# Deviations of the row means made by TensorE and squared by ScalarE, in a convolution whose weights follow from the image

## The reference

```python
def _L0_conv_ref(x, w1, b1, fscale, conv_bias):
    avg = x.mean(axis=(2, 3))
    dyn = avg @ w1.T + b1
    wk = jax.nn.sigmoid(dyn).reshape(b * c, 1, K, K)
    y = lax.conv_general_dilated(xf, wk, ..., feature_group_count=b * c)
    y = y.reshape(b, c, h, w) + conv_bias[None, :, None, None]
    return (x - y) * fs * x + y

def _gn(v, G=32, eps=1e-05):      # one channel per group
    m = jnp.mean(g, axis=(2, 3, 4), keepdims=True)
    s = jnp.var(g, axis=(2, 3, 4), keepdims=True)
    return (g - m) / jnp.sqrt(s + eps)

x = x + _L0_conv_ref(_gn(x), ...)
```

## Time and profile before

| | us |
|---|---|
| median of 3 runs | 265.88 (265.69 to 266.33) |
| profiled execution | 265.87 |
| its span, first to last instruction | 263.9 |
| busy in it: TensorE | 235.7 (89%) |
| VectorE | 231.7 (88%) |
| GpSimd | 227.6 (86%) |
| ScalarE | 211.1 (80%) |

### The profile page before, as it was taken

One profiled execution on the slowest core, in us unless ns is written; L12 is line 12 of the kernel. 1 busy time (PEld: TensorE's weight loads), 2 busy tenths in 40 slices (PEclk: granted clock), 3 DMA queues, 4 the chain that ended last, 5 costly groups with the idle time before them and its releaser, 6 DMA issues.

```text
span 263.9 us, 9720 instructions
## 1 busy us (share of the span) xinstructions
PE 235.7 (89%) x3872; PEld 187.7 (71%) x3872; DVE 231.7 (88%) x552; ACT 211.1 (80%) x389; POOL 227.6 (86%) x259
## 2 busy tenths in 40 slices
PE   0069998989999999989999999999999999999991
PEld 0046875858788786878787887678787878888770
DVE  2886799999999999999999999899999999756655
ACT  2158789797898989797998989697989989899520
POOL 1261579899899999999999999999999999999982
PEclk9999999999999999999999999999999999999997
DMA  7999904696959989797979799797989733444476
GB/s 259 421 422 429 383 4 180 212 401 255 362 236 366 365 280 392 253 390 306 368 288 361 295 366 354 287 386 247 361 325 362 281 160 160 183 181 181 183 290 247
DMA packets 10413, 77.73 MB, mean 295 GB/s; under 512 B 1280, under 2 KB 1408, under 8 KB 2688
## 3 DMA queue, kind: packets, MB, share of 16 engines
q1 hardware_dynamic: 10368, 77.12, 75.8%
HBM read 39.37 MB, written 37.75 MB: 292 GB/s over the span
## 4 chain that ended last, share of the span: by engine, by line
PE 58%; DVE 23%; issue 10%; DMA 3%; ACT 2%; SPq 1%; POOL 1%; DVEq 0%; ACTq 0%; POOLq 0%
PE conv_ps L435 37%; PE conv_ps L441 13%; DVE outs L582 9%; DVE pieces L531 8%; DVE taps L549 4%; PE dyn_ps L419 3%; DMA w1s<-w1r 3%; PE dyn_ps L427 2%; PE conv_ps L497 1%; DVE taps L556 1%; ACT xs L686 1%; ACT linear L722 1%; DVE row_stats L538 1%; PE dyn_ps L404 1%; SPq L314 1%
## 5 line engine op out<-in xcount | busy, mean ns | idle before, releaser
L435 PE MATMUL conv_ps<-xs,taps 64*64 64x448 f32 x1536 | 219.9, 549 | 6.9 <-DVE outs L582 4.3
L852 POOL TENSOR_TENSOR outs<-outs,linear 128x1152 f32<-128x1152 f32 x63 | 166.1, 2647 | 1.0 <-DVE outs L582 0.7
L582 DVE SCALAR_TENSOR_TENSOR outs<-xs,beta,conv_ps 128x576 f32<-128x576 f32 x128 | 102.8, 805 | 20.3 <-PE conv_ps L435 19.6
L435 PEld LDWEIGHTS conv_ps<-xs,taps 64*64 64x64 f32 x1536 | 101.7, 133 | 26.6 <-issue 14.0
L441 PE MATMUL conv_ps<-xs,taps 64*64 64x128 f32 x1536 | 114.3, 272 | 0.6 <-issue 0.6
L722 ACT ACTIVATE linear<-xs,slope 128x576 f32<-128x576 f32 x128 | 109.0, 854 | 3.0 <-POOL outs L852 3.0
L531 DVE BATCH_NORM_STATS2 pieces<-xs 128x6 f32<-128x64 f32 (+1 forms) x256 | 102.2, 447 | 6.0 <-DMA xs<-x 6.0
L441 PEld LDWEIGHTS conv_ps<-xs,taps 64*64 64x64 f32 x1536 | 94.2, 133 | 9.3 <-issue 2.4
L686 ACT ACTIVATE xs<-xs,shift 128x594 f32<-128x594 f32 x128 | 99.2, 778 | 0.0
L809 POOL TENSOR_TENSOR inv_std<-numbers,minus_half 128x8 f32<-128x8 f32 x16 | 26.4, 1649 | 4.8 <-ACT dev_mean L692 4.6
L549 DVE TENSOR_TENSOR taps<-dyn_ps,tap 128x1512 f32<-128x1512 f32 (+1 forms) x19 | 27.8, 1477 | 0.0
(11 more groups left out here) (59 smaller groups left out, 142.0 us busy)
## 6 DMA issues: line engine op xcount, KB each, us to landing
xs<-x SPq DMA_DIRECT2D x30, 1188.0 KB, 11.2
out<-outs SPq DMA_DIRECT2D x30, 1152.0 KB, 5.2
xs<-x SPq DMA_DIRECT2D x4, 594.0 KB, 6.0
out<-outs SPq DMA_DIRECT2D x3, 576.0 KB, 2.8
out<-outs SPq DMA_DIRECT2D x2, 288.0 KB, 2.6
cst<-const SPq DMA_DIRECT2D x1, 275.5 KB, 6.9
w1s<-w1r SPq DMA_DIRECT2D x1, 144.0 KB, 6.8
gates<-gate SPq DMA_DIRECT2D x1, 8.0 KB, 7.0
```

Source lines behind the costliest of these rows:

```text
L435: return nc.tensor.matmul(tile(i, g, taken)[:, START:BANK], taps[given, i % 2, at:at + HALF], xs[given, i % XBUFS, g, 0:PAIRED, 1 + shift: ...
L582: nc.vector.scalar_tensor_tensor(out=outs[:, i % OBUFS, g].rearrange("p (k w) -> p k w", w=COLS), in0=xs[:, i % XBUFS, g, :, 1:1 + COLS], ...
L852: nc.gpsimd.tensor_tensor(tile, tile, linear[:, PAIR * k:PAIR * (k + 1)].rearrange("p g n -> p (g n)"), ALU.add).then_inc(out_ready, 1)
```

## The change

The table of constants gets one more 128 x 128 matrix, "deviate", which is the identity minus "average". Row means times this matrix are the deviations of the row means, so TensorE makes them beside the means: two matmuls more in `mean_even` and two in `mean_odd` (for images 0 and 1 one more over all partitions), into eight columns of PSUM next to the others. ScalarE copies them into `moments`, and squares them into `moments` with a second operation; `negative_mean` waits for the deviations now instead of for the means. The row variance is no longer added to the square: TensorE averages it by itself and accumulates it on the averaged squares, two more matmuls in `spread_even` and two in `spread_odd`. `second_moments` on GpSimd, with its three operations an image, is gone. Statistics lie variance behind mean (`row_stats` with the groups innermost). `mean_even` waits also until the second moments of the image before have been copied, since they share an accumulation region.

```diff
-for _name, _width in (("average", PARTS), ("band", TAPS * HALF), ("turn", TAPS),
+for _name, _width in (("average", PARTS), ("deviate", PARTS), ("band", TAPS * HALF), ("turn", TAPS),
...
+    put("deviate", np.eye(PARTS, dtype=np.float32) - same * new[:, None])
...
-        row_stats = sb("row_stats", [PARTS, 2, GROUPS, 2])
+        row_stats = sb("row_stats", [PARTS, 2, 2, GROUPS])
...
-        square = sb("square", [PARTS, GROUPS])
...
+        dev_ps = stat_ps[:, 3 * GROUPS:4 * GROUPS]
...
-        dev_ready = sem("dev_ready")
-        square_ready = sem("square_ready")
+        dev_done = sem("dev_done")
...
+            def deviate(rows, cols):
+                return const_of("deviate")[rows, cols]
             def mean_even(j):
...
+                pe.wait_ge(zstats_copied, 2 * j)
                 for cols in (TOP, BOTTOM):
-                    nc.tensor.matmul(stat_ps[cols, 0:GROUPS], average(TOP, cols), row_stats[TOP, j % 2, :, 0],
+                    nc.tensor.matmul(mean_ps[cols], average(TOP, cols), row_stats[TOP, j % 2, 0],
                                      start=True, stop=False).then_inc(mean_half, 1)
+                for cols in (TOP, BOTTOM):
+                    nc.tensor.matmul(dev_ps[cols], deviate(TOP, cols), row_stats[TOP, j % 2, 0],
+                                     start=False, stop=False).then_inc(mean_half, 1)
             def mean_odd(j):
-                pe.wait_ge(mean_half, 2 * (j - 1))
+                pe.wait_ge(mean_half, 4 * (j - 1))
                 for cols in (TOP, BOTTOM):
-                    nc.tensor.matmul(stat_ps[cols, 0:GROUPS], average(BOTTOM, cols), row_stats[BOTTOM, j % 2, :, 0],
-                                     start=False, stop=True).then_inc(mean_done, 1)
+                    nc.tensor.matmul(mean_ps[cols], average(BOTTOM, cols), row_stats[BOTTOM, j % 2, 0],
+                                     start=False, stop=False).then_inc(mean_done, 1)
+                for cols in (TOP, BOTTOM):
+                    nc.tensor.matmul(dev_ps[cols], deviate(BOTTOM, cols), row_stats[BOTTOM, j % 2, 0],
+                                     start=False, stop=True).then_inc(dev_done, 1)
             def spread_even(j):
-                pe.wait_ge(moments_ready, j + 1)
+                pe.wait_ge(moments_ready, 2 * (j + 1))
                 for cols in (TOP, BOTTOM):
-                    nc.tensor.matmul(stat_ps[cols, GROUPS:3 * GROUPS], average(TOP, cols),
-                                     moments[TOP].rearrange("p a g -> p (a g)"),
-                                     start=True, stop=False).then_inc(zstats_half, 1)
+                    nc.tensor.matmul(zstats_ps[cols], average(TOP, cols), moments[TOP].rearrange("p a g -> p (a g)"),
+                                     start=True, stop=False)
+                    nc.tensor.matmul(zstats_ps[cols, GROUPS:], average(TOP, cols), row_stats[TOP, j % 2, 1],
+                                     start=False, stop=False).then_inc(zstats_half, 1)
             def spread_odd(j):
...
                 for cols in (TOP, BOTTOM):
-                    nc.tensor.matmul(stat_ps[cols, GROUPS:3 * GROUPS], average(BOTTOM, cols),
-                                     moments[BOTTOM].rearrange("p a g -> p (a g)"),
+                    nc.tensor.matmul(zstats_ps[cols], average(BOTTOM, cols), moments[BOTTOM].rearrange("p a g -> p (a g)"),
+                                     start=False, stop=False)
+                    nc.tensor.matmul(zstats_ps[cols, GROUPS:], average(BOTTOM, cols), row_stats[BOTTOM, j % 2, 1],
                                      start=False, stop=True).then_inc(zstats_done, 1)
             def mean_whole(j):
...
-                nc.tensor.matmul(mean_ps, const_of("average"), row_stats[:, j % 2, :, 0],
-                                 start=True, stop=True).then_inc(mean_done, 1)
+                at_least(pe, zstats_copied, 2 * j)
+                nc.tensor.matmul(mean_ps, const_of("average"), row_stats[:, j % 2, 0],
+                                 start=True, stop=False).then_inc(mean_done, 1)
+                nc.tensor.matmul(dev_ps, const_of("deviate"), row_stats[:, j % 2, 0],
+                                 start=False, stop=True).then_inc(dev_done, 1)
             def spread_whole(j):
-                pe.wait_ge(moments_ready, j + 1)
+                pe.wait_ge(moments_ready, 2 * (j + 1))
...
-                                 start=True, stop=True).then_inc(zstats_done, 1)
+                                 start=True, stop=False)
+                nc.tensor.matmul(zstats_ps[:, GROUPS:], const_of("average"), row_stats[:, j % 2, 1],
+                                 start=False, stop=True).then_inc(zstats_done, 1)
...
-                    ins = nc.vector.bn_aggr(row_stats[:, j % 2, g, :], pieces[:, j % 2, g].rearrange("p h s -> p (h s)"))
+                    ins = nc.vector.bn_aggr(row_stats[:, j % 2, 0:2, g], pieces[:, j % 2, g].rearrange("p h s -> p (h s)"))
...
         def _(act):
-            act.wait_ge(ones_set, 1)
+            act.wait_ge(ones_set, 4)
...
             def negative_mean(j):
-                act.wait_ge(mean_done, j + 1 if j < 2 else 2 * j)
+                act.wait_ge(dev_done, j + 1 if j < 2 else 2 * j)
...
+                nc.scalar.activation(moments[:, 0], dev_ps, ACT.Identity).then_inc(moments_ready, 1)
+                nc.scalar.activation(moments[:, 1], dev_ps, ACT.Square).then_inc(moments_ready, 1)
...
-            def second_moments(j):
-                pool.wait_ge(rows_done, j + 1)
-                pool.wait_ge(neg_mean_ready, j + 1)
-                nc.gpsimd.tensor_tensor(moments[:, 0], row_stats[:, j % 2, :, 0], neg_mean_of(j),
-                                        ALU.add).then_inc(dev_ready, 1)
-                pool.wait_ge(dev_ready, j + 1)
-                nc.gpsimd.tensor_tensor(square[:], moments[:, 0], moments[:, 0], ALU.mult).then_inc(square_ready, 1)
-                pool.wait_ge(square_ready, j + 1)
-                nc.gpsimd.tensor_tensor(moments[:, 1], row_stats[:, j % 2, :, 1], square[:], ALU.add).then_inc(moments_ready, 1)
...
-            second_moments(0)
...
-            second_moments(1)
...
                 add_pair(i, 0)
...
-                if stats and i > 0:
-                    second_moments(i + 2)
...
                 add_pair(i, 1)
-                if i == 0:
-                    second_moments(2)
```

## The result

The changed kernel takes 273.78 us (median, 273.0 to 276.22) against 265.86 for the kernel before in the same comparison: 1.032 times as long, 95% interval 1.028 to 1.037. The forecast of 267.9 us had the sign and a quarter of the size, and its range ended at 270.2.

The account below looks back on a forecast made before the run. It took the bound to be a TensorE–VectorE loop of 14.44 us an image. Added: 0.88 (images 2 to 12), 0.1 (images 0, 1), 0.2 (image 13), 0.86 (start), 2.04 on 265.87: 267.9 us, range 266.2 to 270.2.

Parts of the forecast that it names:

- What bounds the kernel: Image loop of 14.44 us: TensorE to the end of tile 4, VectorE to product 5, then TensorE again.
- The price of the first four matmuls: Deviation matmuls on TensorE before tile 4's end: 0.08 us an image, bounds 0.04 and 0.25; 0.88 over images 2 to 12.
- The rival of the whole overhead: TensorE takes passes in order, each small one costing its whole overhead, 0.25 us an image: 270.1 us; chance 0.18.
- a steady image above 14.65: Sign in the profile after, mid-kernel image time in us, that would show the forecast wrong and whole overhead paid.
- The four spread matmuls: Row variances into second moments on TensorE behind tile 4: no loop cost, under about 0.4 us of cover.
- GpSimd's three operations at 0: Removing GpSimd's operations, 0.74 us an image, gains 0 in the middle, since no chain step stands behind them.
- the rival on it: GpSimd's 14.56 us an image was the long-run pace; freeing it removes long images, 266.6 us; chance 0.20.
- GpSimd's wait for ScalarE's copies: Sign in the profile after: GpSimd waits for ScalarE's copies before its power operation.
- ScalarE: Two added PSUM operations, 0.16 us each, counted at 0; idle before the negative mean falls from 1.2 to about 0.8.
- The start: Serial chain at the kernel's beginning takes all its additions: 0.86 us together, bounds 0 and 1.3.
- The second image's deviations: In the start, they stand on TensorE ahead of the first tile: 0.4 us more, bounds 0 and 0.53.
- The transfer of the weights: In the start, issued behind the constants table, which grows by 65.5 KB: 0.16 us later.

Follow-up runs that it names:

- e1: Kernel before with only the deviations' matmuls added (and the larger table of constants), nobody reading the deviations, GpSimd keeping its operations: 270.65 us.
- e2: Changed kernel without the four deviation matmuls in images 2 to 15, ScalarE using the means in their place: 265.71 us.
- e7: Kernel before with only one pair of deviation matmuls, behind the first pair of means, read by nobody: 270.97 us.
- v2: Kernel before with the dynamic-weight matmuls of images 3 to 15 moved to ahead of tiles 3 and 4: 265.39 us.
- e3: Changed kernel with the two pairs of deviation matmuls moved away from the means, into tiles 4 and 5, still ahead of product 4: 273.44 us.
- e4: Changed kernel with means and deviations in another order of array quarters, same places, each group of four using both row halves: 272.87 us.
- e8: Changed kernel with the first means and deviations half a tile earlier, ahead of the tile's first crossed pair: 271.25 us.
- v1: Changed kernel reworked: mean matmuls carry 32 columns, two added matmuls make deviations, spread matmuls as before, GpSimd regains one small operation: 270.09 us.
- v4: Shared 32-column mean passes with means, deviations and dynamic-weight matmuls moved to other tiles, GpSimd two operations fewer than the kernel before: 265.19 us.

## Why the prediction was wrong

**What bounds the kernel**: right for what was put ahead of product 4. TensorE to product 4, VectorE to product 5, TensorE again is the loop of e1, too, where TensorE waits 0.5 us for VectorE at the image's end. What was put ahead of product 4 lengthened every image by its full size, and e2 shows that nothing else in the change did.

**The price of the first four matmuls**: this is the step that failed, 0.08 forecast and 0.45 measured, eleven times, 4.95 us instead of 0.88. Its bounds, 0.04 and 0.25, came from rows in which small matmuls follow each other or stand one to a quarter, and both are prices per pass. The price here is not of the passes, as e7 shows: it is, by the reading above, mostly the time for which the queue stands until a 448-column pass has ended. The row that could have told it was in the trace of before, in the lines printed above: the mean that starts at 138.40 had waited for its quarter, and the order showed a second matmul for that quarter behind it. "The same instruction in the same place" was true and beside the point.

**The rival of the whole overhead** came nearer (270.1, and 0.18 of the chance), and its sign came, a steady image above 14.65, but for a wrong reason. TensorE does not take all passes in order, as it had it: two passes from behind the waiting mean start at 138.03, ahead of it. The rule of the Trainium skill in "TensorEngine Tiling (Array Packing)", section "Instruction Overhead", some 60 cycles a matmul, would have made the second pair cost as much as the first. Between e7 and e1 the image differs by 0.00 us; only in TensorE's own time, behind product 4, does the second pair show, with 0.09.

**The four spread matmuls** under the cover of 0.4: right as to the loop, e1 and the changed kernel have the same image, but by luck. In TensorE's records tile 6 grows from 1.62 to 2.11 us, by 0.49, and 0.37 without a start stand ahead of these matmuls, too. Tile 7 falls from 2.06 to 1.60, since TensorE no longer waits for VectorE there. They used all of the cover (TensorE busy 14.89 of 14.89) and, with the other four, brought TensorE's records to 530; the stops that come with that, 2.0 us against 1.26, were in no term.

**GpSimd's three operations at 0**: right, e2 with them gone is no faster per image. The drift of GpSimd was no cause of the long image 9, a stop for instructions, so the rival on it falls for this kernel; v2 shows where it becomes true. GpSimd's wait for ScalarE's copies, forecast, is there:

```profile
194.29 1.65 POOL L828 TENSOR_TENSOR inv_std<-numbers,minus_half 128x8 f32<-128x8 f32 x1 [1.02 <-ACT dev_mean L711]
```

**ScalarE**: cost nothing, as counted, but its idle time before the negative mean grew to 1.55 us where 0.8 was forecast, since TensorE's deviations come later. The two added operations start 0.06 us after each other and cost far less than their 0.16 each:

```profile
190.24 0.18 ACT L686 ACTIVATE shift<-stat_ps 128x8 f32<-128x8 f32 x1 [1.55 <-PE stat_ps L374]
190.31 0.17 ACT L687 ACTIVATE moments<-stat_ps 128x8 f32<-128x8 f32 x1
190.37 0.18 ACT L688 ACTIVATE moments<-stat_ps 128x8 f32<-128x8 f32 x1
190.44 0.36 ACT L696 ACTIVATE xs<-shift 128x112 f32<-128x112 f32 x1
```

**The start**: 0.86 forecast, 1.24 measured to the first product. The second image's deviations, the largest term, were right: from the mean (L396) to the next use (L514) it is 0.95 us, 0.53 in the earlier trace rows, so L398 adds 0.42 where 0.4 was counted.

```profile
23.28 0.59 PE L396 MATMUL stat_ps<-row_stats,cst 128*128 128x8 f32 x2
23.72 0.57 PE L398 MATMUL stat_ps<-row_stats,cst 128*128 128x8 f32 x2
24.23 1.17 PE L514 MATMUL conv_ps<-cst 64*128 64x240 f32 x2
25.32 1.01 PE L452 MATMUL conv_ps<-xs,taps 64*64 64x448 f32 x2
```

The transfer of the weights ended no later (at 10.60 us in the chain of waits, 10.81 in the earlier trace rows), so its 0.16 did not show, and from VectorE's first statistics to GpSimd's power operation it takes 0.06 longer, where 0.2 was counted. The first tile itself is longer by more than the 0.1 for the second image's spread matmuls; but the first product moves between executions by as much (29.78 in the kernel before, 29.09 in v2, which has the same start), so one pair of executions does not settle this rest. Over all kernels here the first product comes at 29.73 to 31.02 in the eight with the changed start, 30.43 in the mean, and at 29.09 to 29.78 in the three with the start of before, 29.53 in the mean: a difference of 0.90, near the forecast's 0.86.

**The sum**: forecast 0.88 + 0.1 + 0.2 + 0.86 = 2.04. Measured in the same order: 4.95 in the loop, 0.49 in images 0 and 1, 0.63 from image 13 on, 1.24 in the start, and 0.75 in stops, 8.1 in all.

What stays open: what makes a packet of instructions late, and so why a stop comes in the image in which it comes; and the price of e3. That the queue stops at the second matmul for a busy quarter is the reading that fits e4 to e8 and v1 to v4; the queue itself is in no record.

## What to carry to other kernels

Price an added instruction by what stands in the queue ahead of it, not by its size: on an array used in quarters ask which quarter is busy when it is issued, and whether one for that quarter waits already. When a matmul's price is read from a row of another place, look at that place's order too. And when a change adds instructions to an engine whose list is long and whose waits are few, count them: the fetch of instructions is a resource of the loop.
